# Eight elementwise operations a row change engines in a fused Mamba-and-FFN kernel on one core

## The reference, cut to what matters

```
xx, res = split(x @ in_w.T)                  # 512 channels each
u     = silu(causal_conv4(xx) + conv_b)
delta, B, C = split(u @ xproj_w.T)           # 16 | 16 | 16
delta = softplus(delta @ dt_w.T + dt_b)
carry = exp(delta*A) * carry + delta*B*u     # over the tokens, 16 states a channel
y     = sum_n C_n * carry_n  +  u * D        # u*D: the first product moved here
y     = y * silu(res);   out = y @ out_w.T
```

## Time and profile before

| | |
|---|---|
| median of 3 runs | 2810.76 us |
| range of the 3 runs | 2808.68 to 2812.94 us |
| profiled execution, span | 2810.8 us |
| PE, DVE, ACT, POOL busy | 87%, 86%, 77%, 60% |
| period of an iteration in the middle | 163.0 us |

### The profile page before, as it was taken

How to read it: one execution, slowest core, us unless ns; L and a number is a source line. 1 busy time by engine, 2 the same in 40 slices (tenths; PEclk the granted TensorE clock), 3 DMA queues, 4 the chain that set the end, 5 groups by cost and what they waited for, 6 DMA issues and landing times. The chain is left out here.

```text
span 2810.8 us, 36225 instructions
## 1 busy us (share of the span) xinstructions
PE 2442.6 (87%) x12034; PEld 1851.0 (66%) x12034; DVE 2416.5 (86%) x2379; ACT 2152.1 (77%) x3271; POOL 1676.5 (60%) x1594
## 2 busy tenths in 40 slices
PE   3466898989989899999989899998989999898988
PEld 1334676676767677676767767676766767676767
DVE  4689989998999989999998999999898999989730
ACT  4877796978879697887969787796968779696711
POOL 3553666566566656656655655665665576666544
PEclk7567999999999999999999999999999999999989
DMA  4977898998989898898989889898988989898933
GB/s 155 273 190 171 193 234 195 223 214 204 225 200 233 192 224 214 204 225 201 233 195 224 214 209 219 202 229 200 225 212 208 214 205 228 206 222 203 242 101 117
DMA packets 229262, 581.68 MB, mean 207 GB/s; under 512 B 25920, under 2 KB 26304, under 8 KB 228944
## 3 DMA queue, kind: packets, MB, share of 16 engines
q0 software_dynamic: 73728, 268.47, 52.0%
q1 hardware_dynamic: 118480, 243.71, 25.0%
q10 hardware_dynamic: 36864, 67.13, 8.1%
HBM read 290.32 MB, written 20.45 MB: 111 GB/s over the span
## 5 line engine op out<-in xcount | busy, mean ns | idle before, releaser
L816 DVE TENSOR_TENSOR_SCAN scan_ps<-dA,scan_ps 128x1024 f32<-128x1024 f32 x416 | 951.8, 2288 | 129.9 <-PE scan_ps L422 121.4
L1008 POOL DMA_DIRECT2D y<-hC x512 | 450.6, 880 | 673.3 <-DVE hC L827 555.3
L669 ACT ACTIVATE dB<-duT,bT 128x512 f32<-128x512 f32 x1024 | 715.4, 711 | 76.5 <-PE scan_ps L422 76.4
L422 PE MATMUL scan_ps<-ident,dB 128*128 128x128 f32 x4096 | 577.9, 288 | 153.5 <-DVE hC L827 116.6
L660 ACT ACTIVATE dA<-delta,a_neg 128x512 f32<-128x512 f32 (+1 forms) x1024 | 692.6, 711 | 23.2 <-DVE hC L827 18.2
L535 PE MATMUL ffn_ps<-hb_hi,ring 128*128 128x512 f32 x1536 | 655.0, 426 | 40.9 <-POOL hb_lo L1047 20.6
L422 PEld LDWEIGHTS scan_ps<-ident,dB 128*128 128x128 f32 x4096 | 499.7, 148 | 270.4 <-DVE hC L827 98.6
L535 PE MATMUL ffn_ps<-hb_lo,ring 128*128 128x512 f32 x1536 | 611.6, 398 | 0.0
L827 DVE TENSOR_TENSOR hC<-scan_ps,c_rows_sb 128x1024 f32<-128x1024 f32 x416 | 507.0, 1219 | 37.9 <-DMA y<-hC 9.9
L535 PE MATMUL ffn_ps<-ha_hi,ring 128*128 128x512 f32 x1024 | 438.0, 428 | 7.2 <-POOL ha_lo L1047 4.5
L535 PE MATMUL ffn_ps<-ha_lo,ring 128*128 128x512 f32 x1024 | 403.0, 394 | 0.0
(11 more groups left out here) (100 smaller groups left out, 3241.9 us busy)
## 6 DMA issues: line engine op xcount, KB each, us to landing
y<-hC POOLq DMA_DIRECT2D x512, 512.0 KB, 5.8
ring<-rounded_weights SPq DMA_DIRECT2D x704, 256.0 KB, 4.2
c_rows_sb<-c_rows ACTq DMA_DIRECT2D x256, 256.0 KB, 4.2
x<-ffn_w SPq DMA_DIRECT2D x22, 512.0 KB, 7.2
rounded_weights<-ha_hi SPq DMA_DIRECT2D x22, 512.0 KB, 6.4
xt<-x_chan SPq DMA_DIRECT2D x16, 512.0 KB, 5.6
xt<-x_tok SPq DMA_DIRECT2D x16, 512.0 KB, 4.9
out_st<-x_chan SPq DMA_DIRECT2D x16, 512.0 KB, 4.2
```

The source lines that it names most:

```text
L422: mm = nc.tensor.transpose(dst[:, j * P:(j + 1) * P], src(j), ident[:])
L669: nc.scalar.activation(dB[:, n % 2, t, :], duT[:, t, :], ACT.Copy, scale=bT2[:, par, t, n:n + 1]).then_inc(dB_ready, 1)
L816: nc.vector.tensor_tensor_scan(states, dA[:, a:a + 2, :].rearrange("p a l -> p (a l)"), b, 0.0, ALU.mult, ALU.add).then_inc(scan_done, 1)
L1008: pool.dma_start(y2[:, par, c:c + 2, :], hC[:, slot], accum_op=ALU.add).then_inc(y_added[p % 2], 16)
```

## The change

The four sums w = 1 + e of each row and the four products y2 = u*D of each row are issued by ACT instead of DVE, each at the same step number as before, as ACTIVATE instructions (`Identity` with the bias `ones`, and `Copy` with the scale D). On ACT they stand at the end of the step, behind the `dA` and `dB` tiles, the gelus and the copies of that step. The waits move with them. Nothing else changes.

```diff
-            def front_step(r, par, s, end):
+            def front_step(r, par, s, tail, end):
...
                     nc.scalar.activation(du[:, c, :], du[:, c, :], ACT.Exp, scale=-1.0).then_inc(sp_exp, 1)
+                for c in range(DC):
+                    if F_PLUS[c] != s:
+                        continue
+                    if c == 3:
+                        act.wait_ge(c_stored, r * 16 + 16)
+                        act.wait_ge(pe_bT, r + 1)
+                    if c == 1 and tail is not None:
+                        act.wait_ge(l1_x32, tail * HC + HC)
+                    act.wait_ge(sp_exp, r * DC + (c + 1))
+                    nc.scalar.activation(sp_w[c], du[:, c, :], ACT.Identity, bias=ones[:]).then_inc(sp_plus, 1)
                 if s == F_LN:
...
                     nc.scalar.activation(duT[:, t, :], front_ps(r, t)[:], ACT.Copy).then_inc(duT_ready, 1)
+                for c in range(DC):
+                    if F_Y[c] != s:
+                        continue
+                    act.wait_ge(du_ready, r * DC + (c + 1))
+                    nc.scalar.activation(y2[:, par, c, :], y2[:, par, c, :], ACT.Copy, scale=ch[:, c, C_D:C_D + 1]
+                                         ).then_inc(y_init, 1)
...
-                    if F_PLUS[c] != s:
-                        continue
-                    if c == 3:
-                        dve.wait_ge(c_stored, r * 16 + 16)
-                        dve.wait_ge(pe_bT, r + 1)
-                    if c == 1 and tail is not None:
-                        dve.wait_ge(l1_x32, tail * HC + HC)
-                    dve.wait_ge(sp_exp, r * DC + (c + 1))
-                    nc.vector.tensor_scalar(sp_w[c], du[:, c, :], 1.0, None, ALU.add).then_inc(sp_plus, 1)
...
-                for c in range(DC):
-                    if F_Y[c] != s:
-                        continue
-                    dve.wait_ge(du_ready, r * DC + (c + 1))
-                    nc.vector.tensor_scalar(y2[:, par, c, :], y2[:, par, c, :], ch[:, c, C_D:C_D + 1], None,
-                                            ALU.mult).then_inc(y_init, 1)
```

More of the change, by code:

```diff
@@ L770, in iteration @@
                     if front is not None:
-                        front_step(front, fpar, s, end)
+                        front_step(front, fpar, s, tail, end)
                     t = i * TILES + s
```

## The result

| | median us | range us |
|---|---|---|
| before (4 runs) | 2811.85 | 2808.68 to 2814.89 |
| after (4 runs) | 2863.19 | 2859.81 to 2866.44 |

The ratio is 1.0183 (95% interval 1.0169 to 1.0198): slower, by 51 us. The forecast was 2863. The profiled execution after the change spans 2860.7 us, 49.9 more than the one before.

A forecast was written before the change was run, and what follows sets the result against it. ACT's queue was taken to bound the path from softplus to second gate. Softplus delay 2.1 us plus products, less slack, gave 3.7 us a row; 14 rows made 52 us, 2811 + 52 = 2863 us, range 2836 to 2888.

The forecast's parts named there:

- The direction and the place: Softplus to second gate: slower (88%), since ACT's queue sets the end there and DVE's saved time becomes waiting.
- The price of an operation: Each moved operation: 0.71 us on ACT, 0.61 us with overlap, 4.9 us a row; DVE frees some 4.2 us.
- The step of the softplus: Four sums ahead of the logarithms on ACT: 4 x 0.61 - 0.36 = 2.1 us later, delta and du too.
- The waits along the way: DVE before L868 and L874: waits for ACT rise from 0.18 us a row to some 4.
- The step of the products: Four products with D on ACT: 2.5 us less idle time; ACT 4.1 us late at first tanh, 3.9 by second.
- TensorE at the dB tile: PE's weight load at 1372.46 waits for a dB tile behind seven moved operations, leaving PE 3.5 us late.
- the gate ring: PE's third-group projection, 0.3 us after the second gate frees its buffer: slack off 3.9 leaves 3.6 to 3.7 us.
- The sum: Whole kernel: rows 2 to 15, 14 x 3.7 = 52 us, 2811 + 52 = 2863 us; 58%.
- the two iterations that I had at nothing: Rows 0 and 1, without feed-forward work on ACT: both counted at 0, within 4 us.
- The clock: PE waits more near 1352 to 1359, slowing its clock: up to 3.3 us a row, 2910 us; 12% together with 2884.
- 2884: Rival that all eight operations count in every row: 15 x 4.9 = 74 us; 12% together with the clock.
- The table loads, the C rows and `y_init`: ACT side effects: no table load added; C-row loads up to 4 us later, 0.6 us cover left; `y_init` wait free.

## Why the prediction was right, point by point

*The direction and the place.* Right, and shown: ScalarE's time ahead of the gates is what was paid (1.0171 with nothing else changed), and VectorE's relief was worth some 0.2% (0.9983). DVE's busy share of the span would have said the opposite; the idle time in front of its instructions told which engine it waited for.

*The price of an operation.* 0.72 us against 0.71 expected, 90.1 us in all. By the spacing of neighbours it is 0.61 us: the sum starts at 1359.16 and the next group of ScalarE at 1359.77. The forecasts for the busy totals, 91 us more and 77 us less, forgot the overlap that the price itself had: busy time counts it once, so ScalarE's total rose by 74 us and VectorE's fell by 66, nearer to the 16 x 4.9 = 78 and 16 x 4.2 = 67 of that price.

*The step of the softplus.* Forecast 2.1 us, measured 1.86 at the logarithms and 1.49 at the end of du. I took only the 0.36 us that stands as idle time off the four sums, but a gap has more room than that, since the neighbours beside it don't overlap either. In the kernel before:

```profile
1338.38 0.72 ACT L669 ACTIVATE dB<-duT,bT 128x512 f32<-128x512 f32 x1
...
1347.78 0.71 ACT L669 ACTIVATE dB<-duT,bT 128x512 f32<-128x512 f32 x1
1348.51 0.69 ACT L732 ACTIVATE x<-ffn_ps,fs 128x512 f32<-128x512 f32 x1
...
1363.23 0.72 ACT L669 ACTIVATE dB<-duT,bT 128x512 f32<-128x512 f32 x1
```

From the first of these to the gelu at 1339.47 are 1.09 us, 0.48 more than the 0.61 of neighbours, and from 1347.78 to 1348.51 another 0.12. So 4 x 0.61 - 0.60 = 1.84 us. The rest, down to 1.49, is VectorE's: the first L874 took 1.05 us before and the same operation takes 0.69 us now. In the kernel before it takes 1.05 to 1.06 us in the 14 cases in which GpSimd's L1047 ran beside it and 0.67 to 0.69 in the 50 others; the last L1047 now ends at 1377.60, 0.1 us ahead of it. The waits along the way are as forecast, 3.61 us a row in sum against some 4.

*The step of the products.* I put ScalarE 4.1 us late at the first tanh and 3.9 at the second gate. In the row shown it was 3.5 at the first tanh, by the mean distances 3.90 (50.88 - 46.98), and 3.45 at the second gate (58.24 - 54.79). The gap before the third copy of du, of which I took off 0.3 to 0.7 us, was used up whole: 1.46 us from 1363.23 to 1364.69, 0.85 more than neighbours, and nothing is left of it in the changed kernel. With it the sum for the row shown is 4.88 - 0.60 - 0.85 = 3.43 us. TensorE at the dB tile was 2.7 us late where I had 3.5. It waits 1.70 us for that tile now, so ScalarE's lateness there sets it, 2.9 us by the end of the tile (1399.01 against 1372.20), less some 0.2 us; in the kernel before, VectorE's product ended 0.1 us behind that tile. The slack of 0.3 us in the gate ring is gone as forecast: the projection at 1417.63 waits for the gate that ends at 1417.58. But the mean distances of the third gate and of the period give nothing back for it.

*The sum.* 3.7 us a row forecast, 3.41 measured, by the row shown mainly because the room in ScalarE's gaps was taken too small. 14 rows at 3.41 make 47.7 us instead of 52. Read from the trace, the two iterations that I had at nothing are 1.5 and 2.6 us longer, the 13 periods behind them 44.5, and what follows the last softplus 1.2, where I had counted a full 3.7. The errors nearly cancel in the span (49.9), and the median of 2863.19 against 2863 is closer than the working deserved: that it is met to the microsecond is luck.

*The clock.* The rival was there, and what it cost lies between nothing and 0.3 us a row. (Its 2910 us is the forecast plus 14 x 3.3; on top of 2884 it would have been some 2930.) In the stretch behind the logarithms the clock now falls from its upper level (2.4 GHz) to the lower (1.2) in some rows, which it did not do before. Stages of 10 us from the copy of B on, in two rows after the change, and one row before it:

```profile
1208.80:1218.80 10.00, 7.28 (x39) 5.67 (x36) 7.90 (x10) 9.94 (x17) 3.43 (x4) 1.00 0.92 237
1374.90:1384.90 10.00, 7.47 (x34) 6.04 (x32) 7.90 (x10) 9.89 (x16) 3.43 (x4) 0.83 0.92 238
```
```profile
1349.10:1359.10 10.00, 8.70 (x48) 7.05 (x47) 9.81 (x12) 9.94 (x17) 4.04 (x4) 1.00 0.93 227
```

PE, which has waited 2.53 us for a split there instead of 1.30, is granted 0.83 of full speed over the 10 us of the second row; its matmuls there take 0.63 us each (from 1378.24 on) and 0.39 later. Of 12 rows in the middle 8 have such a stretch; their periods are 166.37 to 166.65 us but for one of 167.67, those of the other four 166.09 to 166.13. That looks like 0.3 us a stretch, at most some 3 us of the 50 (the long period has its third gate at 62.42 like the others, so its extra time comes behind the gates). But in the kernel with the load added on ScalarE, 7 of 13 rows have the same fall to 0.83, and all its periods are 166.19 to 166.25, with it or without. So the fall as such need not cost anything, and what parts the rows of the changed kernel was not found out. I had allowed up to 3.3 us a row.

*The table loads, the C rows and `y_init`.* None was added (196 loads before and after), no wait for `y_init` shows, and the waits for a row of C are two of GpSimd's, 1.3 us together.

*What VectorE's waits before the gates would be.* Forecast some 6 us a row, measured 3.04 + 1.36 = 4.4 in the row shown, and in the whole span 82.3 us for 52.9. The rest is in two waits ahead of the first gate that the forecast doesn't have: 0.96 us for a dA tile and 1.14 us for PE's transposes.

## What to carry to other kernels

Ask of a move between engines which queue is on the path where the work stands, not which engine is fuller over the span: here DVE was busy 86% and ACT 77%, and giving ACT eight operations cost 70% of their time in each row (3.41 of 8 x 0.61 = 4.9 us), while DVE's freed time became waiting. The gaps between the receiving engine's instructions in that stretch are all that it can take in for nothing: here some 1.1 us of idle time, and 1.45 us when the gaps are measured from start to start against the spacing of neighbours. To tell the two sides apart, run the load without the relief and the relief without the load: here they gave 1.0171 and 0.9983, and the change 1.0183.

## What the runs showed of the hardware that was not expected

GpSimd's product with a per-partition scalar took 1.57 us at the median (dB tiles) and 1.56 (products with D, with a mean of 1.79 and single ones up to 3.14) for 128x512 float32, twice its plain cast of that size (0.80 us in the mean in the same runs), against 0.71 us on ScalarE and 0.46 to 1.36 us on VectorE.

VectorE's two times for that product go with what GpSimd does beside it. In the kernel before, L885 took 1.13 to 1.36 us in the 14 cases in which a two-input operation of GpSimd (a TENSOR_TENSOR such as L1047) ran beside it, and 0.46 to 0.49 us in the other 50.

A copy of 128x512 from PSUM takes 0.68 us on VectorE (the kernel with the copies moved) and 0.59 on ScalarE.
